# Two phases of a two-layer decoder joined into one list of work, with a new order around the joint and in phase 2, and one cheaper score step in phase 3

## What is computed

```python
# layer 0                                   16 heads of 16 channels
x = ln(x + causal_attention(x @ Wqkv.T, position bias) @ Wout.T)       # phase 1
x = ln(x + cross_attention_16_heads(x, ctx) @ wo + bo)                 # phase 1
x = ln(x + experts(x))        # 2 shared + 8 routed, 256->128->256     # phase 2
# layer 1
x = ln(x + causal_attention(q, k, v of x) @ w_proj + b_proj)           # phase 2
scores = (x @ Wq + bq) @ (ctx @ Wk + bk).T       # one head            # phase 3
scores = where(mask == 0, -10000, scores)
x = ln(x + softmax(scores) @ v @ Wo + bo)                              # phase 3
x = ln(x + relu(quantum(x @ W1 + b1)) @ W2 + b2)   # 256->1024->256    # phase 3
```

## Time and profile before

| | us |
|---|---|
| median of 3 runs | 3624.97 |
| runs | 3619.38 to 3625.34 |
| profiled execution | 3628.03 |
| its span | 3626.1 |
| TensorE busy | 3344.5 (92%), 20706 matmuls |
| VectorE busy | 2625.4 (72%) |
| ScalarE busy | 2283.5 (63%) |
| GpSimd busy | 1022.4 (28%) |
| chain that ended last | TensorE 71%, ScalarE 11%, VectorE 7%, DMA 5% |

### The profile page before, as it was taken

How to read it: one execution, slowest core, us unless ns; L and a number is a source line. 1 busy time by engine, 2 the same in 40 slices (tenths; PEclk the granted TensorE clock), 3 DMA queues, 4 the chain that set the end, 5 groups by cost and what they waited for, 6 DMA issues and landing times.

```text
span 3626.1 us, 59862 instructions
## 1 busy us (share of the span) xinstructions
PE 3344.5 (92%) x20706; PEld 2528.1 (70%) x20706; DVE 2625.4 (72%) x7153; ACT 2283.5 (63%) x4067; POOL 1022.4 (28%) x1576
## 2 busy tenths in 40 slices
PE   5999999999999848999999999999999876999998
PEld 4677777777777636777777777777777655766664
DVE  5688888888888644677777777777777534788876
ACT  3677777777777622456666555556556543677776
POOL 2244444444444422222222322222223110000000
PEclk8999999999999979999999999999999877999999
DMA  7654545445544021444444444444444421011010
GB/s 193 101 95 84 88 96 107 84 88 95 107 84 82 17 82 53 84 80 77 86 92 94 94 88 88 90 89 93 92 87 88 73 44 62 12 36 35 25 35 24
DMA packets 203403, 283.27 MB, mean 78 GB/s; under 512 B 48929, under 2 KB 131874, under 8 KB 194274
## 3 DMA queue, kind: packets, MB, share of 16 engines
q1 hardware_dynamic: 203106, 279.46, 38.2%
HBM read 179.49 MB, written 96.73 MB: 76 GB/s over the span
## 4 chain that ended last, share of the span: by engine, by line
PE 71%; ACT 11%; DVE 7%; DMA 5%; issue 4%; SPq 1%; POOL 1%; PEld 0%; POOLq 0%; ACTq 0%; PEldq 0%; DVEq 0%
PE ps L829 35%; PE ps L1003 8%; PE ps L978 7%; PE ps L1201 5%; PE ps L1017 5%; ACT q_stack L1669 5%; PE ps L953 3%; DMA qk_scratch<-parts 3%; ACT pt L1686 2%; PE ps L984 1%; PE ps L1077 1%; PE ps L888 1%; PE ps L1028 1%; DMA k_stack<-qk_scratch 1%; DVE nmax L1351 1%
## 5 line engine op out<-in xcount | busy, mean ns | idle before, releaser
L1686 ACT ACTIVATE pt<-ps 128x512 f32<-128x512 f32 x1280 | 735.9, 598 | 346.7 <-PE ps L1003 338.8
L1889 POOL TENSOR_SCALAR_AFFINE_SELECT pt<-pt 128x256 f32<-128x256 f32 x1024 | 392.1, 419 | 704.9 <-ACT pt L1686 704.9
L978 PE MATMUL ps<-k_stack,q_stack 96*128 96x512 f32 (+3 forms) x2048 | 547.2, 338 | 42.3 <-ACT q_stack L1669 11.8
L1358 DVE CUSTOM_DVE_ANT_0 ps<-ps,future 128x512 f32<-128x512 f32 (+3 forms) x1024 | 481.7, 515 | 141.9 <-PE ps L978 138.8
L1003 PE MATMUL ps<-q_stack,k_stack 100*128 100x512 f32 (+3 forms) x2048 | 538.6, 345 | 29.3 <-ACT q_stack L1669 23.4
L1003 PEld LDWEIGHTS ps<-q_stack,k_stack 100*128 100x128 f32 x2048 | 351.5, 195 | 124.9 <-ACT q_stack L1669 37.2
L978 PEld LDWEIGHTS ps<-k_stack,q_stack 96*128 96x128 f32 x2048 | 355.6, 194 | 103.2 <-ACT q_stack L1669 18.8
L1351 DVE TENSOR_REDUCE nmax<-ps 128x1 f32<-128x512 f32 (+2 forms) x768 | 354.4, 502 | 92.0 <-PE ps L984 91.0
L1895 POOL TENSOR_TENSOR rs<-rs 128x4 f32<-128x4 f32 x96 | 97.1, 1012 | 1062.0 <-DVE rs L1394 1062.0
L1669 ACT ACTIVATE q_stack<-ps 4x512 fp32r<-4x512 f32 x512 | 300.8, 588 | 64.7 <-PE ps L992 56.5
L1017 PE MATMUL ps<-pt,v_ones 128*32 128x512 f32 (+3 forms) x4096 | 312.1, 446 | 5.7 <-POOL pt L1889 5.3
(11 more groups left out here) (278 smaller groups left out, 7958.6 us busy)
## 6 DMA issues: line engine op xcount, KB each, us to landing
qk_scratch<-parts SPq DMA_DIRECT2D x64, 1024.0 KB, 5.5
q_stack<-qk_scratch SPq DMA_DIRECT2D x384, 128.0 KB, 4.9
k_stack<-qk_scratch SPq DMA_DIRECT2D x384, 128.0 KB, 5.6
gate_of<-gate_scratch SPq DMA_DIRECT2D x128, 256.0 KB, 5.6
x_mid<-x_ring SPq DMA_DIRECT2D x32, 512.0 KB, 3.9
x_ring<-x_mid SPq DMA_DIRECT2D x32, 512.0 KB, 5.3
x_ring<-in_x SPq DMA_DIRECT2D x16, 512.0 KB, 3.8
out_dram<-x_ring SPq DMA_DIRECT2D x16, 512.0 KB, 2.9
```

The lines of the kernel that those rows point to most:

```text
L978: done = e.matmul(bank(bank_of[piece])[:, at:at + width], a.q[0:96, base + h, t * P:(t + 1) * P], a.k[0:96, base + h, 0:width], start=a.la ...
L1358: done = e.tensor_tensor_reduce(src, src, future[:, SEQ - width:SEQ], -1.0, 3e38, ALU.add, ALU.min, nmax[:, g % 2, to:to + 1])
L1686: e.activation(dst, src, ACT.Exp).then_inc(exp_up.sem)
L1889: done = e.affine_select(out=blk, in_=blk, compare_op=ALU.is_ge, fill=0.0, base=0, pattern=[[0, 2], [1, P]], channel_multiplier=-1)
```

## The change

1. **Phases 1 and 2 are one list.** `walk` has now two parts, `(1, 12)` and `(3, 3)`. The end of phase 1 and the prologue of phase 2 are gone, with their two barriers. Phase 2's due times start at `START[2] = 1198.792` on the clock of phase 1.
2. **Loads and splits of phase 2 become pieces** (`AHEAD`): `rt` (router and two biases), `w2` (five pairs of experts, each one DMA of 768 KB, one split on ScalarE and one on VectorE), `low`, `lw` (the six products for `w_low`), `z` (clearing of the stacks), `wo`. Each waits for the last user of the SBUF it lands in: `w2` for the last `T` of a group of batch 15, `low` for its last `PV`, `z` and `wo` for `tm xw` of batch 15.
3. **Own order for boundary batches** (`EDGE`): batches 13 to 15 of phase 1 and 0 to 2 of phase 2 have due times of their own. In TensorE's list all experts of batch 16+0 and the first experts of the next stand among batches 14 and 15 of phase 1; the first transposes of attention 16 (`tc a1 0`) stand 16 pieces behind `tm xw 15`.
4. **New layout of SBUF**: `v`, `pt`, `oh`, `ol`, `oT`, `o`, `rec` are shared by both layers; the second half of `back2` is `oT`, with waits between `O` and `bk`; PSUM banks are handed out over the joint by one `Banks`.
5. **Phase 2 re-laid**: the period in the table is 93.989 and the order within the period differs. In SyncE's list `send(n, 0)` stands now before `rows` of group 3 of the batch before. The order within a steady period of phase 1 is the same but for one or two neighbouring pieces of TensorE (its table has 73.001), and that of phase 3 is the same (32.104) but for the new `tb`.
6. **Phase 3**: `a_parts` holds high and low part side by side. `cs` makes for each token tile two products with 128 moving columns and two with 64. VectorE copies one half out of PSUM (128x256) and then adds; `q_bias` is folded into `offset` in the prologue, by four VectorE instructions of 128x512 in the place of two of ScalarE. `co_b` is no longer a product but a row added by GpSimd: `tb x1`.

The core of the diff:

```diff
-        for ph in (1, 2, 3):
+        for ph, part in ((1, 12), (3, 3)):
             for engine in ENGINES:
                 first = [("ld", ph, b) for b in range(RING)] if engine == "sync" else []
-                rest = [piece for piece in turns[ph][engine] if piece not in first]
+                rest = [piece for piece in turns[part][engine] if piece not in first]
                 walk[engine] += first + [("prologue", ph)] + rest + [("end", ph)]
...
+def merged(when):
+
+    out = {engine: {**when[1][engine], **ahead_of(engine), **when[2][engine]} for engine in ENGINES}
+    for engine in ENGINES:
+        for batch, rows in EDGE[engine].items():
+            for piece, name, n in named(*batch):
+                if name in rows and rows[name][n] is not None:
+                    out[engine][piece] = rows[name][n]
+    return out
...
+AHEAD = {
+    "tensor": {"lw": [1274.09, 1274.46, 1280.37, 1280.74, 1281.11, 1281.48]},
...
+    "sync": {"w2": [1127.41, 1149.95, 1172.19, 1172.53, 1197.43], "rt": [1107.71], "low": [1200.03], "wo": [1279.18]},
...
+        (2, 0): {
+            "tc a1": [1284.7],
...
+            "tc ex": [1141.67],
...
-            "send": [76.442, 95.983],
-            "rows": [97.435, 117.928, 140.108, 160.952],
...
+            "send": [81.016, 103.64],
+            "rows": [112.618, 134.257, 157.237, 181.688],
...
+                elif kind == "w2":
+                    i, = key
+                    cols = slice(i * 2 * PER_EXPERT, (i + 1) * 2 * PER_EXPERT)
+                    group = ((i + 1) * 2 * PER_EXPERT - 1) // (GROUP * SEQ)
+                    e.wait_ge(*t_up[BATCH - 1, group, UNITS - 1])
+                    e.dma_start(w2_raw[:, cols], dram["w2"][:, cols]).then_inc(w2_in[i], 16)
...
                 elif kind == "cs":
...
-                        ops = []
-                        for c in range(CT):
-                            ops += three(ch[:, c, rows], cl[:, c, rows], a_h[:, c, keys], a_l[:, c, keys])
-                        done = product(e, bank(bank_of[piece])[:, t * CTX:(t + 1) * CTX], ops)
+                        both = bank(bank_of[piece])[:, 2 * t * CTX:2 * (t + 1) * CTX]
+                        done = None
+                        for c, part in ((0, ch), (0, cl), (1, cl), (1, ch)):
+                            wide = part is ch
+                            done = e.matmul(both if wide else both[:, 0:CTX], part[:, c, rows],
+                                            a_parts[:, c, b, :, :].rearrange("p a k -> p (a k)") if wide else a_parts[:, c, b, 0, :],
+                                            start=wide and c == 0, stop=wide and c == 1)
...
-                    ops.append((ones[:, :], co_b[:, :]))
...
-                    e.tensor_tensor(sc3[:, :, :], bank(bank_of[piece])[:, 0:TT * CTX].rearrange("p (t k) -> p t k", t=TT),
-                                    key_row(q_bias), ALU.add).then_inc(cs_add.sem)
+                    halves = bank(bank_of[piece]).rearrange("p (t a k) -> p t a k", t=TT, a=2)
+                    e.tensor_copy(sx3[:, :, :], halves[:, :, 1, :]).then_inc(mine.up())
+                    e.wait_ge(*mine.now)
+                    e.tensor_tensor(sc3[:, :, :], halves[:, :, 0, :], sx3[:, :, :], ALU.add).then_inc(cs_add.sem)
```

More of the change, by code:

```diff
@@ L114, in __init__, with only, marks @@
         self.until = dict.fromkeys(banks, -1e9)
-        self.left = {}
+        self.left, self.mine = {}, list(banks)
+    def only(self, banks):
+        part = Banks(banks)
+        part.until, part.left, part.mine = self.until, self.left, list(banks)
+        return part
+    def marks(self, banks):
+        out = []
+        for bank in banks:
+            if bank in self.left and self.left[bank] not in out:
+                out.append(self.left[bank])
+        return out
     def take(self, mark, until, n=1):
-        firsts = [bank for bank in self.until if bank + n - 1 in self.until and (n == 1 or bank % 2 == 0)]
+        firsts = [bank for bank in self.mine if bank + n - 1 in self.mine and (n == 1 or bank % 2 == 0)]
         first = min(firsts, key=lambda bank: max(self.until[bank + i] for i in range(n)))
@@ L428, in pieces_of @@
         put("tc", "x1", b)
+        put("tb", "x1", b)
         put("cs", b)
@@ new lines, in named @@
+def named(ph, b):
+    place = {}
+    for piece in pieces_of(ph, b):
+        name = piece[0] + (" " + str(piece[1]) if piece[0] in TAGGED else "")
+        place[name] = place.get(name, -1) + 1
+        yield piece, name, place[name]
+def merged(when):
[5 more added lines that the diff above has]
+                    out[engine][piece] = rows[name][n]
+    return out
@@ L450, in times_of @@
     for b in range(BATCH):
[L451 to L454 removed]
+        for piece, name, n in named(ph, b):
             for engine in ENGINES:
@@ L457, in times_of @@
                 if row and row[n] is not None:
-                    out[engine][piece] = b * period + row[n]
+                    out[engine][piece] = START[ph] + b * period + row[n]
     return out
@@ new lines, in low_tiles, with landing @@
+        def low_tiles(n):
+            return [sb(st2, f"w_tile{next(spare)}", [P, DIM], F32R) for _ in range(n)]
+        def landing(name, shape):
+            with ExitStack() as here:
+                return sb(here, name, shape)
+        w2_h = sb(st2, "w2_hi", [P, ALL * PER_EXPERT], F32R)
+        tiles = low_tiles(2)
+        w2_raw = landing("w2_raw", [P, ALL * PER_EXPERT])
+        w2_l = sb(st2, "w2_lo", [P, ALL * PER_EXPERT], F32R)
+        tiles += low_tiles(5)
+        skip(320)
+        gate_of = sb(st2, "gate_of", [P, 2, SEQ])
@@ new lines, in decoder @@
+        att[1].k = [k1_first, sb(st2, "k_stack1b", [P, GROUP, SEQ], F32R)]
+        tiles += low_tiles(4)
+        wo_raw = landing("wo_raw", [P, CT, DIM])
+        tiles += low_tiles(2)
+        st2.close()
+        att[1].share(att[0])
+        back2 = [back2_first, att[1].oT]
+        lgT = back2_first[0:EXPERTS, :]
+        w_low = [[[tiles[(part * 3 + which) * CT + c] for c in range(CT)] for which in range(3)] for part in range(2)]
+        wo1 = [[tiles[12 + part * CT + c] for c in range(CT)] for part in range(2)]
@@ L904, in tensor @@
                         product(e, bank(q), ops).then_inc(kt_up)
-                elif kind == "prologue" and key[0] == 2:
-                    e.wait_ge(low_parts, 2)
-                    for which in range(3):
-                        for c in range(CT):
-                            rows = slice(which * DIM + c * P, which * DIM + (c + 1) * P)
-                            cols = slice(which * DIM, (which + 1) * DIM)
-                            product(e, bank(which * CT + c)[:, 0:DIM], three(
-                                low_h[:, 0, rows], low_l[:, 0, rows],
-                                low_h[:, 1, cols], low_l[:, 1, cols])).then_inc(low_up)
                 elif kind == "prologue" and key[0] == 3:
@@ L937, in tensor @@
                     warm(bank(5)[:, 0:P], 16)
-                if kind == "prologue" and key[0] == 2:
-                    e.wait_ge(w_lo.sem, W3_READY - len(W3.chunks) - 2)
-                    warm(bank(7)[:, 0:P], 20)
                 if kind in ("prologue", "end"):
@@ L955, in tensor @@
                         done.then_inc(tc_up.sem)
+                elif kind == "lw":
+                    which, c = key[0] // CT, key[0] % CT
+                    e.wait_ge(*ahead_lo["low", 0])
+                    for free in left[piece]:
+                        e.wait_ge(*free)
+                    rows = slice(which * DIM + c * P, which * DIM + (c + 1) * P)
+                    cols = slice(which * DIM, (which + 1) * DIM)
+                    product(e, bank(bank_of[piece])[:, 0:DIM], three(
+                        low_h[:, 0, rows], low_l[:, 0, rows], low_h[:, 1, cols], low_l[:, 1, cols])).then_inc(lw_up.sem)
                 elif kind == "qk":
```

695 lines of the change are left out of this document (478 added, 217 removed), and 511 rows, old and new, of tables (AHEAD, EDGE, TABLE).

## The result

| | before | changed kernel |
|---|---|---|
| median | 3623.81 us (4 runs) | 3577.88 us (4 runs) |
| range of the runs | 3619.38 to 3625.34 | 3573.65 to 3581.82 |
| profiled execution | 3628.03 | 3577.31 |
| its span | 3626.1 | 3575.6 |

The ratio is 0.9875 (95% interval 0.9862 to 0.9888). The kernel is faster by 46 us; the forecast was 125 faster (3500), its range 3452 to 3560. The sign was right, the size wrong by a factor of 2.7.

A forecast was written before the change was run, and what follows sets the result against it. TensorE's list was taken to set the time nearly everywhere, with a hole at the joint. 3628.0 − 83 (joint) − 25 (phase 2) − 17 (phase 3) = 3503, less 3 for the median: 3500 us, range 3452 to 3560.

The forecast's parts named there:

- The joint: From ln x0 of batch 12 to ln a1 of batch 1: 609.6 us becomes 527 (500 to 571), so −83.
- B: Joint's middle, ln x0 15 to the first high part of tc a1: from 132.0 to 10 us (6 to 25).
- C: Joint's last part, first high part of tc a1 to ln a1 of batch 1: from 290.6 to 287 us (277 to 301).
- A: Joint's first part, ln x0 12 to ln x0 15: grows from 187.0 to 230 us (217 to 245).
- The third case: Joint gives half (−42): SyncE stands at a w2 or low, or splits delay attentions; 3541 us, chance 0.08.
- The cross-check: Joint from TensorE's useful work at phase 2's busy share, 501 us, plus 28.4 of warm-up transposes: 529 us.
- Phase 2: Send ahead of rows removes ScalarE's wait for its landing: 1.9 us a batch over 13 batches, −25 (0 to −36).
- At least the 1.03: Phase 2: lower figure for the send-first gain, TensorE's 1.03 us wait for ScalarE at the next T.
- the fourth case: Phase 3: GpSimd's tb x1 holds back VectorE ahead of ce, up to +33 us; 3533 us, chance 0.03.
- The +3 of the prologue: Phase 3 prologue: four VectorE instructions of 128x512 replace two of ScalarE, 4 x 0.69 = +3 us.
- no change: Joint doesn't close, as w2 lands behind tm xw 15, and the rest cancels: 3625 us, chance 0.03.
- the rival of phase 2: Phase 2: landing of rows becomes the bound, 11.1 us a batch, +167; slower at 3692 us, chance 0.06.

The follow-up runs named there:

- Experiment 1: Changed kernel with phase 1's last xs in the old bank pair: 3567.92 us; reverse, kernel before with only the new phase 1 due times: 3642.42 us.
- experiment 2: Changed kernel with ScalarE's and VectorE's splits of the router weights (rt) later in their lists: 3577.28 us, joint 555.82 instead of 565.17.
- experiment 4: Changed kernel without the warm-up transposes at the joint: 3561.66 us, joint 548.29.
- experiment 5: Kernel before with only SyncE's send of half 0 put ahead of the rows of group 3 in phase 2: 3619.45 against 3626.76 us.
- experiment 6: Changed kernel with bank, rt and z edits, without joint transposes: 3544.81 us; also without transposes at phase 2's end and phase 3's start: 3550.07. End stretches compared.

## Why the prediction was wrong, step by step

**Phase 1, forecast 0, measured +15.5.** The step that failed is the sentence in the description that due times say nothing but the order, on which the prediction leaves phase 1 out of the sum. The comparison of the two lists found one `xs` and one `S` changed and stopped there. The due times also choose banks. Two pieces per batch in another bank cost 15.5 / 12 = 1.29 us a batch. Experiment 1 shows it in both directions. It could have been seen: the new table stands in the diff, and what reads it is 20 lines of code.

**The joint, forecast −83, measured −44.4.** B (10, measured 14.5) and C (287, measured 288.8) were right. A was 230, with an upper bound of 245, and measured 261.8. Two terms were mis-sized. First, 15 us of the new work were to fill TensorE's gaps; the idle time stayed (23.4 and 25.9), because as much of it was made anew as was filled. The `rt` hole accounts for 10.2 of the 31.8 that A has too much, 6.2 of them idle time (experiment 2). Without it 19.8 us of idle time are left, and no run takes these apart. The prediction looked at the room of ScalarE and VectorE over the whole stretch (118 and 142 us of 196 in the earlier trace rows) and not at whether the data of a split is there when its turn comes. It had written that `rt` and the other loads are put between `kl` with its 20 issues and others; it did not multiply: 20 issues took 11.8 us. "The cost is zero as long as TensorE has the other list's pieces to run" is the false sentence, because a late load doesn't hold up SyncE alone: it holds two engines that TensorE needs for every `S` and `T`. The third case has the size (−42), but not the way: it named SyncE standing at a `w2` or `low`, and had A at 245 and B at 25, where they are 261.8 and 14.5. That its number fits is luck. Second, busy time grew by 72.2 where 58 was counted. Of these 14.2 us, 3.4 are transposes (20.1 to 23.5), 1.4 are two `dn` more than counted (78 products in the trace where 72 were counted, at 0.23), and 4.0 went with the `rt` hole, with the clock. No run splits the other 5.4; the clock of A is 0.97 without the hole, and 0.99 before.

**The cross-check misled.** 529 us agreed with 527 within 2 us, but both had nearly the same assumption in them: that the joint would run with little more idle time than a steady period. The cross-check is 487 of useful work, 28.4 of transposes and 14 of idle time; measured are 496.0, 28.3 and 40.9, so 27 of its 36 us are idle time.

**The transposes** were rightly seen as staying in the list (28.4 counted, 28.3 found), and only that was asked. That 16.9 of them are a cost that the change left behind came out in experiment 4.

**Phase 2, forecast −1.9 a period, measured −0.63.** The mechanism was right and the term mis-sized: ScalarE's wait for the landing has gone from the changed kernel too, but I took the wait of an engine off the path for the gain. "At least the 1.03" was wrong as well: it is one of the long waits, and 0.3 of it stays. What counts is what TensorE waited over many periods, less what stays: the swap is worth 0.42 (experiment 5). The other 0.2 of the changed kernel come with the rest of the new order, of which no run takes a part by itself. TensorE's idle time there fell by 1.2 a period (15.7 to 8.4 over six); the other half of that went into its busy time, which grew by 0.6 a period with the same 3427 records (557.8 to 561.6). Why is open.

**Phase 3** was right in its mechanisms and a little too large: nine periods take 285.90 us (3166.49 to 3452.39) where they took 296.70, −1.2 a batch where 1.4 was counted, and only twelve batches have it, not fourteen (12 x 1.2 = 14.4); `cs` fits to the digit, `co_b` too. `tb x1` held nothing up in the steady batches (the instructions of L2116, with two inputs in SBUF, take 0.691 to 0.695 us in all 128 cases), so the fourth case is out. The copy takes 0.42 (0.45 was counted); of the savings, 0.86 and 0.71, 0.37 a batch is missing, where 0.2 was counted to come through. The +3 of the prologue can't be checked: it lies in the end stretch, whose length varies by 9 us with the clock (experiment 6), so that the agreement of that row of the table (−0.5) says nothing.

**Slower and no change** did not come near: the rival of phase 2 would have shown `ln a1` spaced over 100, and it is 94.97.

The sum, put right with the runs: −83 becomes −44 (of the 39 that are missing A has 32, B 4.5 and C 2; `rt` is 9 of them); −25 becomes −7; +15.5 is new; −17 becomes −15. None of the six cases had more than one of these at a time. The outer bounds of the three terms, −39, 0 and −1, give 3585 together, so the range up to 3560 was narrower than the terms it was made of.

## What to carry to other kernels

When a table of times is replaced, ask of everything that reads it, not only of the order; a buffer picked by a planned release time is a wait in disguise. A load that is moved into a busy stretch is to be followed to the engine that consumes it, with the issues queued ahead of it counted at their measured time, since an engine that waits for late data stops all that stands behind it. And the value of a removed wait is what the bounding engine waited for it over many periods, less what stays behind it, while padding that was put around a barrier has to be questioned when the barrier goes.

## What the runs showed of the hardware that was not expected

A long stretch with gaps takes 369 to 378 us with the same matmul records, at mean granted clocks of 0.85 to 0.81, in seven kernels that differ only before it. With one profile of each it isn't shown whether the kernel sets this or the single execution. An edit of under 10 us before it is hard to judge by the time of the whole kernel; the distance between anchors in the profile tells more.

One pair of rows shows GpSimd holding up VectorE in the changed kernel, in the first batches of phase 3 (it occurs twice):

```profile
3030.58 2.34 POOL L2467 TENSOR_TENSOR x_ring<-x_ring,co_b_rows 128x1024 f32<-128x1024 f32 x1
3030.64 2.30 DVE L1963 SCALAR_TENSOR_TENSOR rs<-ag,rs 128x4 f32<-128x4 f32 x1 [1.13 <-POOL rs L2481]
```

An instruction on four columns takes 2.30 us instead of some 0.16 (the median of the 96) and ends where `tb x1` ends. The Trainium skill ("SBUF — State Buffer", section "Who interferes with whom") states that when VectorE has two inputs in SBUF and GpSimd reads SBUF too, the one that comes second is blocked until the other's instruction is finished; the trace agrees in these two places, with 2.30 us. In the steady batches the order is the other way round: a L2116 of VectorE is in its last 0.2 us when `tb x1` starts, and it is `tb x1` that takes 2.42 to 2.44 instead of 2.34 to 2.37. That is the direction of the rule but under half of the 0.2, so these rows don't show a full block.
